# Cross-attention of layer 1: the DMA engines turn the high half of two tiles of each batch instead of one

## The chip, the cores and the metric

One core of a Trainium2 chip runs the whole program. The metric is the time of one launch on the device in microseconds (us), the median of several runs. Everything below is read from one profiled execution of the kernel before: its own time, its span from the first to the last instruction, and its trace. TensorE appears in it as PE (matmuls) and PEld (weight loads), VectorE as DVE, ScalarE as ACT, GpSimd as POOL, and the queue from which the DMAs are issued (SyncE) as SPq.

## The reference

Two layers of a gated cross-attention block over x of 16 x 56 x 128 and a context of 16 x 1500 x 128. Only the second layer's attention matters here:

```python
# 16 heads of 64, b = 16 batches, lq = 56 queries, lk = 1500 keys
Q = (X @ Wq.T + bq).reshape(b, lq, h, d)
KV = (encoder_out @ Wkv.T + bkv).reshape(b, lk, h, 2 * d)
K, V = (KV[..., :d], KV[..., d:])
scores = jnp.einsum('bqhd,bkhd->bhqk', Q, K) / SCALE
weights = jax.nn.softmax(scores, axis=-1)
attn = jnp.einsum('bhqk,bkhd->bqhd', weights, V).reshape(b, lq, h * d)
out = attn @ Wo.T + bo
```

Layer 0 has an attention of its own and an expert MLP, and layer 1 ends with a quantised MLP. All of it is the same before and after the change.

## The kernel before, in words

**Tiles.** A batch of layer 1 has 16 heads x 56 queries = 896 rows, cut into 7 tiles (T1) of 128 rows, against 1500 keys in 12 chunks of 125. A "group" is a set of tiles whose product with the context is made together: `GROUPS1` is tiles 0 to 3 and tiles 4 to 6. There are 16 batches, so 112 tiles.

**One tile.** PE makes the scores (`pe_scores1`, nine matmuls, L892) into three of the PSUM banks, two sets in turns. DVE takes the row maximum (`dve_max1`, L1573, then a small add, L1577). ACT takes the exponential into `e_row` (`act_exp1`, L1269) and sums the rows. The float32 exponentials are split in two float16 halves: POOL casts the high half (`pool_high1`, L585), and DVE subtracts it to get the low half (`dve_low1`, L1600). Both lie in `halves1`, a ring of two buffers by the tile's parity (named u_w and wg_sb in the trace, whose memory they use). The product with the context wants the halves with keys on the partitions, so both must be transposed, "turned", into `p1[group]`.

**The low halves** are turned by DMA transposes, one for each tile, issued from SyncE in `sync_turn1` (L449). For the first tile of a group SyncE first waits for `pv_done1`: the product of the same group of the batch before must have finished reading `p1[group]`, which the transpose overwrites. After that it waits for `low_done1` of the tile.

**The high halves** are turned by PE, twice six transposes against the identity (`pe_turn1`, L860, u = 0 and 1) into one PSUM bank, and copied out by ACT in two copies (`act_high1`, L1278). The exception is `BY_DMA`, tile 4, the first of the second group: a second DMA transpose turns it, issued right behind the tile's low half (L453), and PE and ACT skip it.

**Rings.** `pool_high1` of tile t writes the buffer of tile t - 2, so it waits until PE has turned that tile. For tile 6 (`BY_DMA + 2`) it waits for the DMA instead, semaphore `high_by_dma1`.

**Order on the engines.** The loop of layer 1 runs over batches and steps t = 0 to 6, written out by hand. In step t, PE makes the scores of tile t + 1, turns the high half of tile t - 1 and does a part of a group's product (`pe_pv1`, L912): the first group's 12 chunks lie in steps 5 and 6 and in steps 0 and 1 of the next batch, the second group's in steps 2 to 4. In step 1 all of the part comes before the second six transposes. Step 4, like step 0, begins behind the scores with a small transpose of the row sums' inverses (`pe_inverse1`, L884), which waits for both ACT copies of the tile turned in the step before. In step 6 of every second batch PE also makes a projection (L868). DVE's order in step t is: in steps 2 and 5 the scaling of a finished product (`dve_scale1`, L1591), then maximum of tile t + 1, reciprocal of the sum of tile t (L1582), low half of tile t. ACT's order in step t is: first copy of tile t - 1, exponential of tile t + 1, second copy of tile t - 1. POOL only casts, tile after tile. SyncE's order: low half of each tile as above, and between them the inverses' way to DRAM and back (L461, L469), the next batch's context (L423, L430).

**How long.** Layer 1's attention runs from about 640 to 1190 us of the span. A pair of batches takes some 68 us: in the pair that serves as the pattern here, step 1 of the first batch begins at 817.34 us and step 2 at 821.86 us, and step 2 of the second one at 853.93 us.

Of the kernel before, what the change touches and what calls it, by code (L numbers as in the profile page):

```python
# [27 lines left out]
def flamingo_kernel(nc, x, ctx_in, mask, g_xattn, g_ffn,  # L28
                    wv0, wk0, wq0, wo0, bo0, gate_w, sh_gate, sh_up, sh_down, rt_gate, rt_up, rt_down,
                    wq1, bq1, wkv1, bkv1, wo1, bo1, w_gate, w_up, w_down, out):  # L30
    B, S, E = x.shape
# [20 lines left out]
    T1 = ROWS // 128  # L52
# [17 lines left out]
    with ctx:  # L70
# [158 lines left out]
        GROUPS1 = [(0, 4), (4, T1)]  # L229
# [199 lines left out]
            part = slice(4 * third, 4 * third + 4)  # L429
            sp.dma_start(c_keep1[par][:, part], split_rows[b, :, part]).then_inc(sem(f"kept1_{par}"), 16)  # L430

        BY_DMA = GROUPS1[1][0]

        def turns_till(b, t):

            return b * (T1 - 1) + (t if t <= BY_DMA else t - 1)

        def turned1(b, par, t):

# [2 lines left out]
        def sync_turn1(sp, b, par, t):  # L442

            grp = 0 if t < GROUPS1[1][0] else 1
            first = GROUPS1[grp][0]
            if t == first:
                wait_apart(sp, "sp", (sem("pv_done1"), 4 * (b - 1) + 2 * grp + 2))
            wait_apart(sp, "sp", (sem("low_done1"), b * T1 + t + 1))
            sp.dma_start_transpose(p1[grp][:, 1, :, 128 * (t - first):128 * (t - first + 1)],  # L449
                                   halves1[(t + par) % 2][:, 1].rearrange("p c k -> p (c k)"))\  # L450
                .then_inc(turned1(b, par, t)[0], 16)
            if t == BY_DMA:
                sp.dma_start_transpose(p1[grp][:, 0, :, 128 * (t - first):128 * (t - first + 1)],  # L453
                                       halves1[(t + par) % 2][:, 0].rearrange("p c k -> p (c k)"))\
                    .then_inc(sem("high_by_dma1"), 16)
# [124 lines left out]
        def pool_high1(pool, b, par, t):  # L580

            wait_apart(pool, "pool", (sem("exp_done1"), b * T1 + t + 1), (sem("turned_high1"), 2 * turns_till(b, t - 1)))
            if t == BY_DMA + 2:
                wait_apart(pool, "pool", (sem("high_by_dma1"), 16 * (b + 1)))
            pool.tensor_copy(halves1[(t + par) % 2][:, 0, :, 0:KP], e_row[(t + par) % 2][:].rearrange("p (c k) -> p c k", c=KC))\  # L585
                .then_inc(sem("high_done1"), 1)

# [262 lines left out]
        def pe_turn1(pe, b, par, t, u, after_proj=False):  # L850

            if u == 0:
                pe.wait_ge(sem("high_done1"), b * T1 + t + 1)
            wait(pe, sem("high_copied1"), 2 * turns_till(b, t) + u)
            if after_proj:
                pe.wait_ge(sem("block_done1"), b)
            if isinstance(b, int) and b == B - 1 and t in (3, BY_DMA + 1) and u == 0:
                pe.wait_ge(sem("residual"), 2 * TT + (4 if t == 3 else EARLY))
            for c in range(UC):
                last = pe.transpose(turned_half1()[:, 128 * c:128 * (c + 1)], halves1[(t + par) % 2][:, 0, UC * u + c, :],  # L860
                                    ident16[:])
            last.then_inc(sem("turned_high1"), 1)
# [34 lines left out]
        def pe_pv1(pe, b, par, grp, first, end):  # L897

            a, z = GROUPS1[grp]
            cols = 128 * (z - a)  # L900
            if first == 0:
                for t in (z - 2, z - 1):
                    pe.wait_ge(*turned1(b, par, t))
                pe.wait_ge(sem("high_copied1"), 2 * turns_till(b, z))
                if grp == 1:
                    pe.wait_ge(sem("high_by_dma1"), 16 * (b + 1))
                wait(pe, sem("u_scaled1"), 2 * b + grp)
                if grp == 0:
                    pe.wait_ge(sem(f"kept1_{par}"), per_use(b, par, 48))
            for c in range(first, end):  # L910
                for cl, pl in ((0, 0), (0, 1), (1, 0)):
                    last = pe.matmul(bank[:, U_BANK, 0:cols], c_keep1[par][:, c, cl, :], p1[grp][0:KP, pl, c, :],  # L912
                                     start=(c == 0 and cl + pl == 0), stop=(c == KC - 1 and cl == 1))
                if c in (UC - 1, KC - 1):
                    last.then_inc(sem("pv_done1"), 1)

        @block.tensor
        def _(pe):
# [221 lines left out]
            def layer1(b, par, first, last):  # L1140
                for t in range(T1):
                    if t < T1 - 1:
                        pe_scores1(pe, b, par, t + 1)
                    elif not last:
                        pe_scores1(pe, b + 1, 1 - par, 0)
                    turn = (b, par, t - 1) if t > 0 else (b - 1, 1 - par, T1 - 1)
                    has_turn = not (first and t == 0) and t - 1 != BY_DMA
                    proj = t == T1 - 1 and par == 0 and not first
                    if t >= 5:
                        product = (b, par, 0, 3 * (t - 5), 3 * (t - 4))  # L1150
                    elif t < 2:
                        product = (b - 1, 1 - par, 0, 3 * (t + 2), 3 * (t + 3))
                    else:
                        product = (b - 1, 1 - par, 1, 4 * (t - 2), 4 * (t - 1))
                    has_product = t >= 5 or not first
                    middle = product[4] if t == 1 else product[3] + (3 if t in (0, 4) else 2)
                    if t == 0 and not first:
                        pe_inverse1(pe, b - 1, 1 - par, 1)
                    if t == 4:
                        pe_inverse1(pe, b, par, 0)  # L1160
                    if t in (0, 4) and has_product:
                        pe_pv1(pe, *product[:4], product[3] + 1)
                        product = (*product[:3], product[3] + 1, product[4])
                    if t == 4 or t == 0 and not first:
                        pe.wait_ge(sem("inverse_row1"), 2 * b + t // 4)
                    if proj:
                        pe.wait_ge(sem("high_copied1"), 2 * turns_till(b, t - 1))
                        pe_proj1(pe, b)
                    elif has_turn:
                        pe_turn1(pe, *turn, 0)  # L1170
                    if has_product:
                        pe_pv1(pe, *product[:4], middle)
                    if has_turn:
                        pe_turn1(pe, *turn, 0 if proj else 1, proj)
                    if has_product and middle < product[4]:
                        pe_pv1(pe, *product[:3], middle, product[4])
                    if proj:
                        pe_turn1(pe, *turn, 1)
                    if last and t in (3, 4):
                        pe.wait_ge(sem("high_copied1"), 2 * turns_till(b, t))  # L1180
                        pe_block_turn(pe, B - 2, range(4) if t == 3 else range(4, EARLY), early_turned, "block_done1")
# [90 lines left out]
        def act_high1(act, b, par, t, u):  # L1272
            grp = 0 if t < GROUPS1[1][0] else 1
            at = t - GROUPS1[grp][0]
            act.wait_ge(sem("turned_high1"), 2 * turns_till(b, t) + u + 1)
            if t in (0, BY_DMA + 1):
                wait(act, sem("pv_done1"), 4 * (b - 1) + 2 * grp + u + 1)
            act.copy(p1[grp][:, 0, UC * u:UC * (u + 1), 128 * at:128 * (at + 1)],  # L1278
                     turned_half1().rearrange("p (c r) -> p c r", c=UC)).then_inc(sem("high_copied1"), 1)
# [19 lines left out]
        def _(act):  # L1299
# [149 lines left out]
            def layer1(b, par, first, last):  # L1449
                for t in range(T1):  # L1450
                    if t == 0 and not first:
                        act_inverse1(act, b - 1, 1)
                    if t == 4:
                        act_inverse1(act, b, 0)
                    turn = (b, par, t - 1) if t > 0 else (b - 1, 1 - par, T1 - 1)
                    has_turn = not (first and t == 0) and t - 1 != BY_DMA
                    proj = t == T1 - 1 and par == 0 and not first
                    if proj:
                        act_block1(act, b)
                    elif has_turn:  # L1460
                        act_high1(act, *turn, 0)
                    if t < T1 - 1:
                        act_exp1(act, b, par, t + 1)
                    elif not last:
                        act_exp1(act, b + 1, 1 - par, 0)
                    if proj:
                        act_high1(act, *turn, 0)
                    if has_turn:
                        act_high1(act, *turn, 1)
# [421 lines left out]
```

## Time and profile before

| | before |
|---|---|
| median of 3 runs | 1237.04 us (1234.59 to 1239.03) |
| the profiled execution, its own time | 1237.67 us |
| its span | 1235.9 us |
| PE busy | 1121.8 us, 91% of the span |
| DVE busy | 890.4 us, 72% |
| ACT busy | 674.8 us, 55% |
| POOL busy | 519.8 us, 42% |
| chain that ended last, by engine | PE 73%, DVE 12%, ACT 6% |
| turns of the high halves, L860 | PE 192 groups of six, ACT 192 copies of 794 ns |
| DMA transposes | 128, 3.8 to 3.9 us from issue to landing (median) |

In the timeline every row has its start in us from the span's beginning, the duration in us, the engine, the line, the operation, the output and input by the program's names, the count of instructions merged into the row, and in brackets the idle time just before it with what ended it. Matmuls are pipelined, so that the duration of a group on PE reaches some 0.2 us into the next one; the cost of a group on PE is the distance between starts. A row of SPq lasts as long as the queue is taken by the issue, not until the transfer lands.

### The profile page before, as it was taken

How to read it: one execution, taken by the hardware profiler on the slowest of the kernel's cores; microseconds unless marked ns; L12 is line 12 of the kernel's file. 1: busy time of each engine (PE TensorE's matmuls, PEld its weight loads, DVE VectorE, ACT ScalarE, POOL GpSimd, SP SyncE). 2: the span in 40 equal slices, each digit the busy share in tenths (PEclk: the TensorE clock that was granted, in tenths of full speed). 3: DMA queues.
4: the chain of work that ended last, by engine and by line, in shares of the span. 5: the costliest groups of instructions: out<-in, count | busy, mean ns of one | idle time of the engine just before them, and what ended most of it. 6: DMA issues, size and time to landing. Idle time of an engine off the chain costs nothing.

```text
span 1235.9 us, 27523 instructions
## 1 busy us (share of the span) xinstructions
PE 1121.8 (91%) x9862; PEld 639.0 (52%) x9864; DVE 890.4 (72%) x1242; ACT 674.8 (55%) x935; POOL 519.8 (42%) x352
## 2 busy tenths in 40 slices
PE   4789999999999979878887999999999999999984
PEld 2255556566665645634433555555555555555542
DVE  7766666666666673587787887878787878878768
ACT  2345555555555545545575656656565656566532
POOL 8546675666666653432213332322232322323220
PEclk9889999999999999699998999999999999999996
DMA  3456555545555461000006887868776776768640
GB/s 105 121 169 197 169 168 165 156 149 160 157 178 158 145 159 47 20 1 26 2 0 130 161 164 142 158 140 163 137 163 144 156 162 141 159 141 160 131 79 16
DMA packets 247351, 157.59 MB, mean 128 GB/s; under 512 B 209664, under 2 KB 220400, under 8 KB 247296
## 3 DMA queue, kind: packets, MB, share of 16 engines
q1 hardware_dynamic: 247008, 156.86, 54.1%
q8 instruction: 34, 0.56, 0.2%
q14 instruction: 21, 0.17, 0.0%
q10 hardware_dynamic: 288, 0.00, 0.0%
HBM read 62.23 MB, written 25.39 MB: 71 GB/s over the span
## 4 chain that ended last, share of the span: by engine, by line
PE 73%; DVE 12%; issue 7%; ACT 6%; DMA 1%; SPq 0%; POOL 0%; ACTq 0%; DVEq 0%; another core or an unknown queue 0%; POOLq 0%
PE bank L892 16%; PE bank L912 15%; PE bank L767 7%; PE bank L791 6%; PE bank L860 5%; PE bank L795 5%; PE bank L808 4%; DVE region L1716 2%; PE bank L868 2%; PE bank L934 2%; DVE neg_max L1573 2%; ACT region L1242 2%; DVE e_row L1534 2%; PE bank L1135 2%; PE bank L1097 2%
## 5 line engine op out<-in xcount | busy, mean ns | idle before, releaser
L1534 DVE CUSTOM_DVE_ANT_0 e_row<-bank,region 112x1500 f32<-112x1500 f32 x128 | 220.1, 1719 | 125.5 <-PE bank L767 124.2
L1242 ACT ACTIVATE region<-bank 125x896 f32<-125x896 f32 x192 | 176.0, 917 | 203.8 <-PE bank L795 203.7
L1573 DVE TENSOR_REDUCE neg_max<-bank 128x1 f32<-128x1500 f32 x112 | 192.6, 1720 | 111.8 <-PE bank L892 111.8
L892 PE MATMUL bank<-region 128*128 128x500 f16 x1008 | 235.3, 379 | 3.2 <-ACT e_row L1269 1.8
L1269 ACT ACTIVATE e_row<-bank,neg_shift 128x1500 f32<-128x1500 f32 x112 | 169.2, 1511 | 101.0 <-DVE neg_shift L1577 58.4
L1278 ACT COPY region<-bank 128x768 f16<-128x768 f16 x192 | 152.4, 794 | 72.3 <-PE bank L860 72.3
L585 POOL CAST u_w<-e_row 128x1500 f16<-128x1500 f32 x56 | 83.0, 1483 | 209.4 <-ACT e_row L1269 179.2
L585 POOL CAST wg_sb<-e_row 128x1500 f16<-128x1500 f32 x56 | 83.1, 1484 | 192.4 <-ACT e_row L1269 128.4
L892 PEld LDWEIGHTS bank<-region 128*128 (+1 forms) x1008 | 97.4, 98 | 108.0 <-issue 3.5
L791 PE MATMUL bank<-row_of,region 112*128 112x448 bf16 x384 | 137.8, 359 | 7.6 <-ACT region L1242 7.6
L795 PE MATMUL bank<-region 97*128 (+1 forms) x768 | 137.6, 260 | 0.0
L912 PE MATMUL bank<-region 125*128 125x384 f16 (+1 forms) x576 | 126.1, 352 | 0.0
L912 PE MATMUL bank<-region,g_w 125*128 125x384 f16 (+1 forms) x576 | 124.8, 352 | 0.2 <-DMA region<-wg_sb 0.2
L646 POOL TENSOR_SCALAR region<-region 112x1500 bf16<-112x1500 int32 x16 | 105.3, 6583 | 35.3 <-PE bank L795 29.2
L767 PE MATMUL bank<-region 96*128 96x500 f16 x384 | 105.9, 385 | 12.5 <-DVE neg_max L1534 6.8
L808 PE MATMUL bank<-region 125*32 125x112 f32 x3072 | 113.1, 266 | 0.0
L795 PEld LDWEIGHTS bank<-region 97*128 97x128 f16 x768 | 76.0, 99 | 43.3 <-issue 0.9
L1600 DVE TENSOR_TENSOR u_w<-e_row,u_w 128x1500 f16<-128x1500 f32 x56 | 95.7, 1709 | 3.2 <-DMA region<-u_w 1.6
L1600 DVE TENSOR_TENSOR wg_sb<-e_row,wg_sb 128x1500 f16<-128x1500 f32 x56 | 95.5, 1706 | 3.1 <-POOL wg_sb L585 3.0
L808 PEld LDWEIGHTS bank<-region 125*32 125x32 f32 x3072 | 67.7, 109 | 41.0 <-issue 34.6
L912 PEld LDWEIGHTS bank<-region,g_w 125*128 125x128 f16 x576 | 52.8, 97 | 38.8 <-issue 1.3
L912 PEld LDWEIGHTS bank<-region 125*128 125x128 f16 x576 | 52.9, 97 | 38.5 <-issue 1.1
(218 smaller groups left out, 1495.3 us busy)
## 6 DMA issues: line engine op xcount, KB each, us to landing
region<-region SPq DMA_DIRECT2D x192, 96.0 KB, 2.2
turned_rows<-region SPq DMA_DIRECT2D x16, 768.0 KB, 3.8
region<-turned_rows SPq DMA_DIRECT2D x32, 384.0 KB, 3.5
c_in<-in_ctx SPq DMA_DIRECT2D x16, 750.0 KB
split_rows<-region SPq DMA_DIRECT2D x16, 750.0 KB
region<-in_mask_Bx1xSxS_if SPq DMA_DIRECT2D x32, 328.1 KB
region<-split_rows SPq DMA_DIRECT2D x24, 250.0 KB
g_w<-split_rows SPq DMA_DIRECT2D x24, 250.0 KB
```

Of the source, the lines that this page charges most:

```text
L585: pool.tensor_copy(halves1[(t + par) % 2][:, 0, :, 0:KP], e_row[(t + par) % 2][:].rearrange("p (c k) -> p c k", c=KC))\
L767: last = pe.matmul(bank[:, k, 0:4 * KP], q0_flat[0:96, bass.ds(b * ROWS + R0 * t, 128)], c_stack[par][0:96, t // 2, 4 * k:4 * k + 4, 0:KP] ...
L791: pe.matmul(into[:, 0:HALF_ROWS], mask_flat[par][:, KP * c:KP * c + 128], row_of[:].rearrange("p h s -> p (h s)"), start=True, stop=False)
L795: last = pe.matmul(into[:, GC * g:GC * (g + 1)], c_stack[par][0:97, 2 * h + g, c, :], q0[0:97, b, rows:rows + GC], start=False, stop=(g == 1))
L808: pe.matmul(bank[32 * j:32 * j + 32, U_BANK, 0:R0], c_pv[par][:, c, 4 * h + j, :], p0[:, c, R0 * j:R0 * (j + 1)], start=(c == 0), stop=False)
L892: last = pe.matmul(score_banks1(par, t)[:, k, :], q1[:, ql, b, 128 * t:128 * (t + 1)], c_t1[par][:, cl, 4 * k:4 * k + 4, 0:KP], start=(ql ...
L912: last = pe.matmul(bank[:, U_BANK, 0:cols], c_keep1[par][:, c, cl, :], p1[grp][0:KP, pl, c, :], start=(c == 0 and cl + pl == 0), stop=(c = ...
L1242: act.activation(p0[:, 2 * i:2 * i + 2, :], ring0("s", h, i)[0:KP, :, 0:HALF_ROWS], ACT.Exp, scale=SCALE0)\
L1269: act.activation(e_row[(t + par) % 2][:].rearrange("p (a k) -> p a k", a=3), score_banks1(par, t), ACT.Exp, bias=neg_shift[:, t:t + 1], ac ...
L1534: dve.tensor_tensor_reduce(out=masked.rearrange("p (a k) -> p a k", a=3), in0=bank[0:R0, 0:3, 0:4 * KP], in1=mask_bias[par][:].rearrange(" ...
L1573: dve.tensor_reduce(neg_max[:, t:t + 1], score_banks1(par, t), AX.XY, ALU.max, negate=True)\
L1600: dve.tensor_tensor(half[:, 1, :, 0:KP], e_row[(t + par) % 2][:].rearrange("p (c k) -> p c k", c=KC), half[:, 0, :, 0:KP], ALU.subtract).t ...
```

## The change

`BY_DMA` becomes a list of the first tile of each group, tiles 0 and 4. So tile 0's high half, too, is turned by a DMA transpose that SyncE issues right behind that of its low half. PE's twelve transposes and ACT's two copies for tile 0 go away, the counts of turned tiles follow (5 for each batch instead of 6), POOL's cast of tile 2 waits for the DMA of tile 0 as that of tile 6 does for tile 4, the first group's product waits for the DMA as well, and ACT's wait for free space in `p1[0]` moves from tile 0 to tile 1. The order of everything else is kept.

```diff
-        BY_DMA = GROUPS1[1][0]
+        BY_DMA = [first for first, _ in GROUPS1]
         def turns_till(b, t):
-            return b * (T1 - 1) + (t if t <= BY_DMA else t - 1)
+            return b * (T1 - len(BY_DMA)) + t - len([d for d in BY_DMA if d < t])
+        def turned_by_dma(b, grp):
+            return sem("high_by_dma1"), 16 * (b * len(BY_DMA) + grp + 1)
@@ sync_turn1
-            if t == BY_DMA:
+            if t in BY_DMA:
                 sp.dma_start_transpose(p1[grp][:, 0, :, 128 * (t - first):128 * (t - first + 1)],
                                        halves1[(t + par) % 2][:, 0].rearrange("p c k -> p (c k)"))\
                     .then_inc(sem("high_by_dma1"), 16)
@@ pool_high1
-            if t == BY_DMA + 2:
-                wait_apart(pool, "pool", (sem("high_by_dma1"), 16 * (b + 1)))
+            if t - 2 in BY_DMA:
+                wait_apart(pool, "pool", turned_by_dma(b, BY_DMA.index(t - 2)))
@@ pe_pv1
-                if grp == 1:
-                    pe.wait_ge(sem("high_by_dma1"), 16 * (b + 1))
+                pe.wait_ge(*turned_by_dma(b, grp))
@@ the loops of PE and ACT
-                    has_turn = not (first and t == 0) and t - 1 != BY_DMA
+                    has_turn = not (first and t == 0) and t - 1 not in BY_DMA
@@ act_high1
-            if t in (0, BY_DMA + 1):
+            if t - 1 in BY_DMA:
                 wait(act, sem("pv_done1"), 4 * (b - 1) + 2 * grp + u + 1)
```

## Rows read from the trace of the kernel before

**Rows 1.** Windows: PE, PEld, DVE, ACT, POOL busy, then PEclk, DMA share, GB/s.
```profile
700.00:1170.00 470.00, 464.40 (x3097) 257.12 (x3096) 364.77 (x414) 284.38 (x393) 143.23 (x97) 1.00 0.76 151
```
**Rows 2.** Timeline, PE and SPq around step 1 of a batch (first of a pair).
```profile
817.34 2.08 PE L892 MATMUL bank<-region 128*128 128x500 f16 x9
...
819.25 0.50 PE L860 MATMUL bank<-ident,wg_sb 128*128 128x128 f16 x6
...
821.53 0.50 PE L860 MATMUL bank<-ident,wg_sb 128*128 128x128 f16 x6
821.86 2.08 PE L892 MATMUL bank<-region 128*128 128x500 f16 x9
...
821.95 1.32 SPq L449 DMA_TRANSPOSE region<-wg_sb  x1
...
823.46 1.77 SPq L449 DMA_TRANSPOSE region<-u_w  x1
```
**Rows 3.** Timeline, the same batch: tile 4's DMA transpose and POOL's cast of tile 6.
```profile
838.46 1.79 SPq L453 DMA_TRANSPOSE region<-wg_sb  x1
...
840.47 0.64 SPq L461 DMA_DIRECT2D inverse_rows<-place  x1
...
842.72 1.44 POOL L585 CAST wg_sb<-e_row 128x1500 f16<-128x1500 f32 x1 [4.22 <-DMA region<-wg_sb]
...
843.72 0.44 DVE L1577 TENSOR_TENSOR neg_shift<-neg_max,lift 128x1 f32<-128x1 f32 x1
...
844.19 1.72 DVE L1600 TENSOR_TENSOR wg_sb<-e_row,wg_sb 128x1500 f16<-128x1500 f32 x1
```
**Rows 4.** Timeline, a DMA transpose of tile 4 (batch 2) and the cast it released.
```profile
733.95 1.85 SPq L453 DMA_TRANSPOSE region<-u_w  x1
...
739.60 1.44 POOL L585 CAST u_w<-e_row 128x1500 f16<-128x1500 f32 x1 [5.32 <-DMA region<-u_w]
```
**Rows 5.** Timeline, steps 2 to 4 of the batch of rows 2.
```profile
823.25 1.44 POOL L585 CAST wg_sb<-e_row 128x1500 f16<-128x1500 f32 x1 [3.21 <-ACT e_row L1269]
...
827.77 1.44 POOL L585 CAST u_w<-e_row 128x1500 f16<-128x1500 f32 x1 [3.09 <-ACT e_row L1269]
...
828.44 0.50 PE L860 MATMUL bank<-ident,wg_sb 128*128 128x128 f16 x6
...
828.64 1.72 DVE L1573 TENSOR_REDUCE neg_max<-bank 128x1 f32<-128x1500 f32 x1 [1.06 <-PE bank L892]
...
831.15 2.08 PE L892 MATMUL bank<-region 128*128 128x500 f16 x9
...
833.07 0.27 PE L884 MATMUL bank<-ident,row_inv 128*4 128x128 f32 x1
```
**Rows 6.** Timeline, layer 0: two POOL instructions in a row, other buffers.
```profile
42.09 3.10 POOL L639 TENSOR_TENSOR region<-c_in,region 125x1536 f16<-125x1536 f32 x1
45.13 1.57 POOL L654 COPY region<-c_in 125x1536 f32<-125x1536 f32 x1
```
**Rows 7.** Timeline, batch 2, steps 2 to 4: a low half that came late.
```profile
723.05 1.72 DVE L1600 TENSOR_TENSOR u_w<-e_row,u_w 128x1500 f16<-128x1500 f32 x1 [1.59 <-DMA region<-u_w]
...
729.05 0.27 PE L884 MATMUL bank<-ident,row_inv 128*4 128x128 f32 x1 [0.40 <-ACT region L1278]
```
**Rows 8.** Timeline, steps 2 to 4 of the other kind of batch (second of a pair).
```profile
854.01 1.45 SPq L449 DMA_TRANSPOSE region<-u_w  x1
...
855.65 1.63 SPq L449 DMA_TRANSPOSE region<-wg_sb  x1
...
865.43 0.27 PE L884 MATMUL bank<-ident,row_inv 128*4 128x128 f32 x1
```
**Rows 9.** Timeline, PE in batch 0: nine score matmuls at the lower clock.
```profile
655.57 3.55 PE L892 MATMUL bank<-region 128*128 128x500 f16 x9
```
**Rows 10.** Windows as in rows 1: two stretches of batch 0 in which PE idles.
```profile
651.80:655.00 3.20, 0.49 (x6) 0.35 (x6) 3.17 (x5) 2.52 (x5) 1.44 (x1) 1.00 0.59 112
...
644.25:646.05 1.80, 0.00 (x0) 0.00 (x0) 1.77 (x3) 1.60 (x2) 0.00 (x0) 1.00 0.00 0
```

More of the change, by code:

```diff
@@ L856, in pe_turn1 @@
                 pe.wait_ge(sem("block_done1"), b)
-            if isinstance(b, int) and b == B - 1 and t in (3, BY_DMA + 1) and u == 0:
+            if isinstance(b, int) and b == B - 1 and t in (3, BY_DMA[1] + 1) and u == 0:
                 pe.wait_ge(sem("residual"), 2 * TT + (4 if t == 3 else EARLY))
@@ L1455, in layer1 @@
                     turn = (b, par, t - 1) if t > 0 else (b - 1, 1 - par, T1 - 1)
-                    has_turn = not (first and t == 0) and t - 1 != BY_DMA
+                    has_turn = not (first and t == 0) and t - 1 not in BY_DMA
                     proj = t == T1 - 1 and par == 0 and not first
```

## The prediction, as it was put on record before the run

> **What bounds the kernel now.** The page first: PE is busy for 91% of the span and holds 73% of the chain that ended last. Layer 1's attention can then be looked at alone in the windows: in 470 us of it PE is busy for 464.4 us, at the full clock, while DVE has 364.8, ACT 284.4 and POOL 143.2 us [rows 1]. So in this stage work taken off PE is time gained, as long as nothing makes PE wait. The reader should see one more thing there: PE has no idle time to give, so every us that it is made to wait is a us lost, and this is the side on which the change has to be judged. For that the timeline is the right view, step by step, and in it the order of SyncE, POOL and DVE around the tile whose turn moves.
>
> **What the change removes.** PE's cost of a group of six transposes is the distance from its start to the next start: 821.53 to 821.86, so 0.33 us [rows 2]. Tile 0 has two groups, 0.66 us for each batch. One stands before the end of the first group's product in step 1, the other behind it. Over 16 batches that is 10.6 us, all on PE, which bounds. ACT's two copies were beside PE's work (ACT has 284.4 of 470 us [rows 1]) and I count them at nothing: they are hidden by PE's scores and products, and without that cover they would be worth 0.8 us each by the table.
>
> **What it adds: an issue.** SyncE issues a second transpose behind tile 0's low half. The place matters. Tile 0's low half is not issued when it is ready but when `pv_done1` lets it, at the end of step 1: 821.95, beside the start of step 2 on PE at 821.86 [rows 2]. The added issue therefore starts at the end of step 1 as well. It takes the queue for some 2.0 us, as tile 4's does (838.46 to 840.47 [rows 3]). Queued behind it are tile 1's low half (before at 823.46 [rows 2], now some 1.7 us later), the inverses of the batch before and the next context. The next tile's low half that DVE makes comes several us later, by which time the queue is free again, so I count the issue itself at nothing; were that slack gone, the 2.0 us would be its price in a batch.
>
> **What it adds: a wait, and who stands behind it.** POOL's cast of tile 2 overwrites tile 0's high half and now waits for the DMA to land. For tile 4 the same wait ends 4.26 us after the issue begins (838.46 to 842.72 [rows 3]); the longest such distance is 5.65 us, in batch 2 [rows 4]. I take 4.26, which is that of the steady batches, and keep 5.65 for the range; the lower bound would be a landing that is there before POOL asks, a cost of nothing. For batch 0, whose `pv_done1` wait is void, I give 1 us in all.
>
> Step by step in the batch of rows 2, all starts as before up to 817.34:
> - The product ends 0.33 us sooner, so tile 0's low half is issued at 821.95 - 0.33 = 821.62 and the high half 1.51 us later (the distance of two neighbouring transposes, 821.95 to 823.46 [rows 2]), at 823.13.
> - It has landed, and POOL begins tile 2's cast, at 823.13 + 4.26 = 827.39. Before, it began at 823.25 [rows 5], with nothing to wait for. The cast ends at 828.83 (1.44 us).
> - Tile 3's exponential is ready by then: its cast stood at 827.77 before [rows 5]. So two casts follow each other on POOL, tile 2's and tile 3's. The casts' successors: DVE wants to make tile 2's low half as soon as the first one is done. In the trace DVE starts 0.03 us after the end of the cast (842.72 + 1.44 = 844.16, start 844.19 [rows 3]). POOL starts its next instruction, when its waits are long fulfilled, 0.06 us before the end of the one before by the modelled spans (42.09 + 3.10 = 45.19, start 45.13 [rows 6]). So POOL comes first.
> - A DVE instruction that comes second waits for POOL: the small add beginning at 843.72 lasts 0.44 us, to 844.16, exactly the end of the cast that runs beside it [rows 3]. So the low half cannot run beside tile 3's cast: 828.83 + 1.44 + 1.70 gives 831.97 for its end, rather than 830.56.
> - Behind the low half stand, on DVE, the maximum of tile 4, then on ACT its exponential and the second copy of tile 2, then on PE the small transpose L884 of step 4. That chain can be read where a low half came late: 723.05 + 1.72 = 724.77 to 729.05, so 4.28 us, and the row says that PE idled for ACT there [rows 7]. So L884 starts at 836.25, against 833.07 before [rows 5]: **3.18 us** later in this batch.
>
> In the other kind of batch the same steps give: 854.01 - 0.33 = 853.68, issue of the high half 1.64 us later at 855.32, landing 859.58, end of the second cast 862.46, low half 864.16, L884 at 868.44, against 865.43 [rows 8]: **3.01 us**. The mean is 3.1 us. The 0.66 us that PE saves lie within it, since they are before L884. From L884 on DVE is no longer late against PE: the maximum of tile 4 came at 828.64 only because it waited for PE [rows 5], and such waits take up the rest. The next batch starts as late as this one ended, and PE cannot win it back. 15 batches have the `pv_done1` wait: 15 x 3.1 = 46.5 us.
>
> **A page of the Trainium skill on this step.** "SBUF — State Buffer", section "Who interferes with whom", says that a DVE instruction with two SBUF inputs contends with a GpSimd instruction that reads SBUF, and that whoever issues first holds the shared ports for the whole instruction. The low half has two such inputs and the cast reads SBUF; the small add of rows 3 agrees. By this rule the sum stays at 3.1 us a batch; without any contention it would be the 1.7 us of the first rival.
>
> **What it adds: the clock.** PE idles within the batch: turn of tile 2 at 828.9 instead of 828.44 [rows 5], then the scores of tile 5 at 828.9 + 2.71 (828.44 to 831.15) = 831.6, over at 833.5 (831.15 to 833.07), and nothing to do until 836.25, some 2.7 us. In batch 0 a stretch of 3.20 us with 0.49 us of PE work was followed by nine score matmuls in 3.55 us at the lower of the two clock levels, 1.2 instead of 2.4 GHz, against 2.08 us [rows 9, 2]: 1.47 us lost. A stretch of 1.80 us with no work kept the clock [rows 10]. Our 2.7 us lie between, so the price of a batch is between 0 and 1.47 us; nearer to the longer one, but I take half, 0.7 us: 15 x 0.7 = 10.5 us.
>
> **The sum.** 46.5 + 10.5 + 1 = 58 us on the profiled execution's own 1237.67 us (span 1235.9 and 1.8 around it), which stands 0.6 us above the median: 1237.04 + 58 = **1295 us**.
>
> **The rivals.**
> - **DVE comes before POOL** at the hand-over. Then the low half ends at 830.56 and L884 starts at 834.84, 1.77 us late; 1.60 us in the other kind; mean 1.7. The idle stretch is 1.3 us, short enough to keep the clock [rows 10]. 15 x 1.7 = 25.5, with batch 0 1264 us. For it: only 0.1 us separates the two starts, and the POOL row is from another stage. Against it: all else in the trace has POOL's waits served ahead.
> - **The landing is hidden, and the kernel gets faster.** The place is POOL's wait before tile 2's cast. L884 stays at 833.07 if the low half ends by 828.79, so if the high half lands by 828.79 - 1.70 - 1.44 = 825.6, that is 2.5 us after its issue at 823.13. Below that the 0.66 us begin to count; if the landing is early enough, 16 x 0.66 = 10.6 us are gained: 1226 us. It would also need DVE and ACT to keep up with the shorter step. For it: tile 4's turn by DMA costs PE nothing, since its low half is issued early in its step. Against: every landing in rows 3 and 4 took over 4 us.
> - **The landing is as slow as in batch 2** in every batch, since tile 1's transpose is issued close behind: 1.39 us more, 15 x 1.39 = 21 us, 1316 us. Against it: tile 1's transpose stands behind in the same queue.
> - **Nothing to be seen**, as the wait costs just what PE saves: within 0.3%, that is 1233 to 1241 us. It needs a landing some 2.5 us after the issue in every batch, for which no row speaks.
> - That the change does not remove the turns is no rival: the loops of PE and ACT skip tile 0 by the same test that skips tile 4.
>
> **How the numbers follow.** POOL first, with the clock's cost anywhere between none and full (1285 to 1307 us): 0.64. DVE first: 0.20. Slower landing: 0.05. Hidden: 0.07. Nothing to be seen: 0.04. A difference of about 0.3% is what a measurement of this kernel can tell from no change; so slower 0.89, same 0.04, faster 0.07. The range for 8 in 10 runs from the DVE-first case, 1260, to the full price of the clock with some of the slower landing, 1312.
>
> **What the profile after would show.** POOL's cast of tile 2 released by the DMA in every batch, some 4 us later against the end of step 1. The cast of tile 3 directly behind it; DVE's low half of tile 2 with some 3.1 us instead of 1.7 if POOL comes first, 1.7 if not. PE's idle time before L884 of the first group some 2.7 us (1.3 in the rival) and named as waiting for ACT, and about 0.5 to 1 us before the turn of tile 2. Nine-matmul groups of over 3 us if the clock falls. Steps 5, 6, 0 unchanged, step 1 shorter by 0.66 us. The prediction is wrong if the high half lands within 2.5 us, or if `pv_done1` is not what holds the first issue back.

## The result, and the profile after

| | before | after |
|---|---|---|
| median | 1237.51 us (1234.59 to 1239.03, 4 runs) | 1293.38 us (1291.48 to 1305.89, 4 runs) |
| the profiled execution, its own time | 1237.67 us | 1295.08 us |
| its span | 1235.9 us | 1293.4 us |
| PE busy | 91% | 87% |
| chain that ended last: PE, DVE, DMA | 73%, 12%, 1% | 60%, 13%, 5% |

The ratio is 1.0462, with a 95% interval of 1.0408 to 1.0516: the change makes the kernel 4.6% slower. One of the five runs of experiment 2 below took 1614.97 us at a granted clock of 0.65, where the others have 0.97, and is left out of its ratio. The line numbers after are 3 to 4 higher than before (L884 is now L888, L892 is L896, L585 is L589, L912 is L915).

The window that rows 1 show, in the kernel after (columns as there):

```profile
700.00:1170.00 470.00, 424.42 (x2641) 229.01 (x2638) 341.08 (x377) 240.99 (x332) 125.04 (x88) 0.97 0.74 148
```

PE is busy for 424 of 470 us instead of 464, and no other engine has taken its place: all of them do less in the same time. So the engines wait for each other, and the waits of PE, with total, number and longest, name for whom in that window:

```profile
PE bank L888 <- ACT region L1281: 30.5, 14, 2.4
PE bank L864 <- POOL u_w L589: 5.1, 6, 1.1
PE bank L864 <- POOL wg_sb L589: 4.9, 6, 0.8
...
PE bank L915 <- DVE region L1594: 2.4, 12, 0.2
```

L888 is the small transpose of the row sums' inverses. Thirteen of its fourteen waits lie in step 4, one for each batch of the window, and take 2.22 to 2.39 us each; the other, 1.02 us, lies in step 0 once. Before, this wait was 1.6 us in all. ACT is only the last link. The timeline of a batch shows the whole chain (first kind, to be laid beside rows 2 and 5; step 1 begins at 835.80):

```profile
835.80 2.08 PE L896 MATMUL bank<-region 128*128 128x500 f16 x9
...
840.08 1.44 SPq L453 DMA_TRANSPOSE region<-wg_sb  x1
...
841.57 1.80 SPq L457 DMA_TRANSPOSE region<-wg_sb  x1
...
845.87 1.44 POOL L589 CAST wg_sb<-e_row 128x1500 f16<-128x1500 f32 x1 [7.36 <-DMA region<-wg_sb]
...
847.25 1.44 POOL L589 CAST u_w<-e_row 128x1500 f16<-128x1500 f32 x1
847.34 2.92 DVE L1603 TENSOR_TENSOR wg_sb<-e_row,wg_sb 128x1500 f16<-128x1500 f32 x1 [3.33 <-POOL wg_sb L589]
847.45 0.51 PE L864 MATMUL bank<-ident,wg_sb 128*128 128x128 f16 x6 [0.82 <-POOL wg_sb L589]
...
850.18 1.71 DVE L1576 TENSOR_REDUCE neg_max<-bank 128x1 f32<-128x1500 f32 x1
...
854.46 0.27 PE L888 MATMUL bank<-ident,row_inv 128*4 128x128 f32 x1 [2.22 <-ACT region L1281]
```

Read from the top: SyncE issues the low half where the product lets it, then the high half; POOL has idled 7.36 us when that has landed; two casts follow each other without a gap, DVE's low half starts 0.09 us behind the second and needs 2.92 us instead of 1.70; maximum, exponential and copy follow; PE has idled 2.22 us at L888. From the start of step 1 to L888 it takes 18.66 us, against 15.73 us before (817.34 to 833.07 [rows 2, 5]): 2.93 us more. In the other kind of batch it is 872.10 to 890.82, 18.72 us against 16.03 us (849.40 to 865.43 [rows 8]): 2.69 us more.

The rest lies behind L888, and only in the first kind, in PE's work of step 4:

```profile
855.50 2.03 PE L915 MATMUL bank<-region 125*128 125x384 f16 x6
857.33 0.85 PE L864 MATMUL bank<-ident,u_w 128*128 128x128 f16 x6
857.97 1.17 PE L915 MATMUL bank<-region 125*128 125x384 f16 x3
```

In the second kind the same three take 1.14, 0.51 and 0.65 us. The granted clock, the number before the last two, is at its lower level from 856 to 859 us and back behind it:

```profile
856.00:859.00 3.00, 3.00 (x15) 1.78 (x14) 1.29 (x1) 2.79 (x4) 0.66 (x1) 0.50 0.92 204
859.00:860.00 1.00, 1.00 (x6) 0.46 (x5) 0.56 (x1) 0.01 (x1) 0.78 (x1) 0.99 0.00 0
```

From L888 to step 1 of the next batch it takes 17.64 us (854.46 to 872.10) against 16.33 us before (833.07 to 849.40): 1.31 us more. In the second kind it is 20.14 against 20.15 us. So a pair of batches costs 2.93 + 1.31 + 2.69 = 6.93 us more. The distances of L888 say the same: 75.2 us for a pair (36.4 and 38.8) against 68.25.

From the first L888 of a group-0 product to the last it is 567.8 us against 512.8: 55.0 of the 57.4 us that the two profiled executions differ by. What stands ahead of the first (batch 0) is 2.7 us longer and what stands behind the last is not longer (59.4 against 59.6 us).

### The profile page after: what moved, and what is told of

Its sections match the earlier page's. It is cut to its first block, busy times and chain, and to the rows that moved or that the text cites. A ratio compares the mean times of both kernels' runs of the same rounds, so it can differ in the third digit from the quotient of the medians.

```text
span 1293.4 us, 27104 instructions
## 1 busy us (share of the span) xinstructions
PE 1128.8 (87%) x9672; PEld 635.1 (49%) x9672; DVE 905.5 (70%) x1242; ACT 650.8 (50%) x903; POOL 515.1 (40%) x352
## 4 chain that ended last, share of the span: by engine, by line
PE 60%; DVE 13%; issue 11%; ACT 6%; DMA 5%; POOL 2%; SPq 2%; DVEq 0%; ACTq 0%; POOLq 0%
PE bank L915 12%; PE bank L896 9%; PE bank L771 7%; PE bank L795 5%; PE bank L799 5%; PE bank L812 4%; PE bank L864 3%; DMA region<-wg_sb 3%; DVE neg_max L1576 3%; DMA region<-u_w 3%; DVE e_row L1537 2%; DVE region L1719 2%; ACT region L1245 2%; PE bank L872 2%; PE bank L937 2%
## 5 line engine op out<-in xcount | busy, mean ns | idle before, releaser
L896 PE MATMUL bank<-region 128*128 128x500 f16 x1008 | 236.9, 381 | 3.3 <-ACT e_row L1272 1.8
L589 POOL CAST u_w<-e_row 128x1500 f16<-128x1500 f32 x56 | 80.6, 1439 | 233.9 <-ACT e_row L1272 174.8
L589 POOL CAST wg_sb<-e_row 128x1500 f16<-128x1500 f32 x56 | 81.8, 1461 | 228.2 <-DMA region<-wg_sb 101.7
L1281 ACT COPY region<-bank 128x768 f16<-128x768 f16 x160 | 127.2, 795 | 72.6 <-PE bank L864 72.5
L896 PEld LDWEIGHTS bank<-region 128*128 (+1 forms) x1008 | 98.4, 99 | 113.5 <-issue 6.2
L915 PE MATMUL bank<-region 125*128 125x384 f16 (+1 forms) x576 | 134.1, 369 | 1.6 <-DVE region L1594 1.6
L915 PE MATMUL bank<-region,g_w 125*128 125x384 f16 (+1 forms) x576 | 125.9, 354 | 1.4 <-DVE region L1594 1.4
L1603 DVE TENSOR_TENSOR wg_sb<-e_row,wg_sb 128x1500 f16<-128x1500 f32 x56 | 105.2, 1878 | 27.7 <-POOL wg_sb L589 27.7
L1603 DVE TENSOR_TENSOR u_w<-e_row,u_w 128x1500 f16<-128x1500 f32 x56 | 104.9, 1873 | 26.9 <-POOL u_w L589 26.9
L915 PEld LDWEIGHTS bank<-region 125*128 125x128 f16 x576 | 55.8, 102 | 45.3 <-issue 7.7
L915 PEld LDWEIGHTS bank<-region,g_w 125*128 125x128 f16 x576 | 53.4, 98 | 42.5 <-DVE region L1594 2.2
```

Of the source, the lines that this page charges most:

```text
L896: last = pe.matmul(score_banks1(par, t)[:, k, :], q1[:, ql, b, 128 * t:128 * (t + 1)], c_t1[par][:, cl, 4 * k:4 * k + 4, 0:KP], start=(ql ...
L1603: dve.tensor_tensor(half[:, 1, :, 0:KP], e_row[(t + par) % 2][:].rearrange("p (c k) -> p c k", c=KC), half[:, 0, :, 0:KP], ALU.subtract).t ...
```

## The experiments

The ratios are to the kernel before.

**1. The hand-over from POOL to DVE.** POOL's cast of tile 3 waits, in the changed kernel, until DVE has made tile 2's low half.

```diff
+            if t == 3:
+                wait_apart(pool, "pool", (sem("low_done1"), b * T1 + 3))
             pool.tensor_copy(halves1[(t + par) % 2][:, 0, :, 0:KP],
...
```

> The changed kernel, and POOL's cast of tile 3 also waits until DVE has made tile 2's low half, so that DVE comes first at the hand-over. Theory (the time lies in POOL's wait for the landing, 1.4 us a batch more in the hand-over, and some 0.65 us a batch in the clock that the long idle stretch costs): the low half takes 1.7 instead of 2.9 us, L888 idles about 0.9 instead of 2.3 us, the clock holds; 15 x 1.4 + 10 = 31 us less than the changed kernel's 1293, so 1262. Rival (the order at the hand-over is hidden, the landing alone counts): no change, 1293.

Measured: 1264.01 us, ratio 1.0222 (1.0189 to 1.0254). 29 us of the 56 are gone by adding a wait. The low half and L890 (L888 there) of the same kind of batch:

```profile
835.11 1.72 DVE L1605 TENSOR_TENSOR wg_sb<-e_row,wg_sb 128x1500 f16<-128x1500 f32 x1 [3.36 <-POOL wg_sb L591]
...
837.00 1.44 POOL L591 CAST u_w<-e_row 128x1500 f16<-128x1500 f32 x1 [1.93 <-DVE wg_sb L1605]
...
841.03 0.27 PE L890 MATMUL bank<-ident,row_inv 128*4 128x128 f32 x1 [1.02 <-ACT region L1283]
```

The idle time before L890 is 1.02 and 1.19 us in the two kinds. From L890 to L890 a pair of batches takes 71.3 us (33.7 and 37.6) instead of 75.2, and no groups at the lower clock are left in the steady batches; 15 x 3.9 / 2 = 29 us. So the order at the hand-over, with the clock that hangs on it, makes half the loss: that is shown.

**2. The wait on POOL.** Tile 0's high half is cast into a buffer of its own, which nobody overwrites in the same batch. Both transposes are issued where they were.

```diff
         carve([128, KC, 2, E], F16)
+        spare_high = region[:, split_at:split_at + KC * 64].bitcast(F16).rearrange("p (c k) -> p c k", c=KC)
...
+        def high1(par, t):
+            return spare_high if t == 0 else halves1[(t + par) % 2][:, 0]
@@ pool_high1
-            if t - 2 in BY_DMA:
+            if t == 0:
+                wait_apart(pool, "pool", turned_by_dma(b - 1, 0))
+            if t - 2 in BY_DMA[1:]:
...
```

The cast, the subtraction and the transpose of tile 0 then take `high1(par, t)` as their buffer.

> The changed kernel, but tile 0's high half lies in a buffer of its own, so that POOL's cast of tile 2 has nothing to wait for; both DMA transposes, their place in the queue and the product's wait for them stay. Theory (only the wait costs): PE keeps the 0.66 us a batch, less some 0.2 us in which step 2's product now waits for DVE's scaling; 1237.5 - 15 x 0.46 to 0.66 = 1227 to 1231. Rival (the second transpose itself costs, by traffic or by holding SyncE's queue): 1250 or more.

Measured: 1225.81 us, ratio 0.9904 (0.9878 to 0.9931). The same kernel again, with more runs:

> The changed kernel with tile 0's high half in a buffer of its own once more, in more rounds, for the interval: 1226 us, ratio 0.990 to the kernel before.

Measured: 1226.62 us, ratio 0.9905 (0.9874 to 0.9936). The transposes cost nothing; the wait on POOL was the whole loss and more. The window of rows 1 in this kernel, and PE's waits in it:

```profile
700.00:1170.00 470.00, 459.87 (x2971) 251.33 (x2969) 369.31 (x424) 269.43 (x371) 141.43 (x98) 1.00 0.82 164
```

```profile
PE bank L922 <- DVE region L1601: 2.7, 14, 0.2
...
PE bank L895 <- ACT region L1288: 1.3, 6, 0.3
```

PE is back at 460 us, the DMA share rose to 0.82, and L895 (L888 there) waits 1.3 us in all. What is left is a wait of 0.2 us a batch for DVE's scaling in step 2.

**3. The removal alone.** Tile 0's high half is turned by nobody (its place in `p1` holds zeros), and neither POOL nor the product waits for it.

```diff
@@ sync_turn1
-            if t in BY_DMA:
+            if t == 4:
                 sp.dma_start_transpose(p1[grp][:, 0, ...
@@ pool_high1
-            if t - 2 in BY_DMA:
+            if t - 2 == 4:
...
@@ pe_pv1
-                pe.wait_ge(*turned_by_dma(b, grp))
+                if grp == 1:
+                    pe.wait_ge(*turned_by_dma(b, 1))
...
```

> The changed kernel without tile 0's high transpose and without any wait for it: tile 0's high half is turned by nobody (its place in p1 holds zeros), so that this is the removal alone. Theory: 1227 to 1231, within 2 us of the kernel with the buffer of its own, since the issue and the traffic of the transpose are hidden. Rival (issue and traffic cost something): this kernel is faster than that one by over 4 us.

Measured: 1226.83 us, ratio 0.9912 (0.9882 to 0.9942), the same as experiment 2 within the intervals. So the issue on SyncE and the 384 KB through the DMA engines are hidden, as far as a difference of about 4 us in all, or 0.25 us a batch, can be told.

**4. The high half first.** Tile 0's two transposes change places in the queue.

```diff
+            def low():
+                sp.dma_start_transpose(p1[grp][:, 1, :, 128 * (t - first):128 * (t - first + 1)],
...
+            if t != 0:
+                low()
             if t in BY_DMA:
                 sp.dma_start_transpose(p1[grp][:, 0, :, 128 * (t - first):128 * (t - first + 1)],
...
+            if t == 0:
+                low()
```

> The changed kernel with tile 0's high half issued ahead of its low half. The high half lands 1.5 us sooner, the low half (for which DVE's low half of tile 2 waits, being in the same buffer) 1.5 us later. Theory: POOL casts tile 2 some 1.5 us sooner; if tile 3's exponential is ready by then, POOL again comes first and the gain is 15 x 1.5 + 10 for the clock = 32 us, 1261; if DVE comes first, 15 x 2.9 + 10 = 53 us, 1240. Rival (POOL's wait is not what binds): 1293.

Measured: 1249.28 us, ratio 1.0104 (1.0072 to 1.0136), between the two numbers of the theory. The timeline shows both of its cases, one in each kind of batch:

```profile
861.70 1.72 DVE L1608 TENSOR_TENSOR u_w<-e_row,u_w 128x1500 f16<-128x1500 f32 x1 [1.63 <-DMA region<-u_w]
861.97 2.75 POOL L594 CAST wg_sb<-e_row 128x1500 f16<-128x1500 f32 x1 [0.54 <-ACT e_row L1277]
...
867.70 0.27 PE L893 MATMUL bank<-ident,row_inv 128*4 128x128 f32 x1 [0.44 <-ACT region L1286]
...
897.88 1.44 POOL L594 CAST u_w<-e_row 128x1500 f16<-128x1500 f32 x1 [0.44 <-ACT e_row L1277]
897.97 2.92 DVE L1608 TENSOR_TENSOR wg_sb<-e_row,wg_sb 128x1500 f16<-128x1500 f32 x1 [1.91 <-DMA region<-wg_sb]
...
905.09 0.27 PE L893 MATMUL bank<-ident,row_inv 128*4 128x128 f32 x1 [1.78 <-ACT region L1286]
```

In the first DVE comes 0.27 us before POOL, needs 1.72 us, and POOL's cast stretches to 2.75; PE idles 0.44 us. In the second POOL comes 0.09 us before DVE, which needs 2.92 us, and PE idles 1.78 us. PE's idle time differs by 1.3 us between the kinds, and in the second one POOL's lead was only 0.09 us. The kinds differ in more than the order, though; the next experiment gives both the same order.

**5. Both orders together:** the edits of experiments 1 and 4.

> The changed kernel with both orders changed: tile 0's high half issued ahead of its low half, and POOL's cast of tile 3 behind DVE's low half of tile 2. With the high half first alone 1249 us was measured, POOL coming first in one kind of batch (2.92 us low half, 1.78 us idle before L888) and DVE in the other (0.45 us idle). Theory: both kinds behave like the second one, so the pair takes some 1.2 us less and the clock holds: 1249 - 8 x 1.2 = 1239. Rival (the two orders do not add): 1249 or more.

Measured: 1238.07 us, ratio 0.9991 (0.9966 to 1.0016). In the kind in which POOL had come first:

```profile
973.86 1.72 DVE L1610 TENSOR_TENSOR wg_sb<-e_row,wg_sb 128x1500 f16<-128x1500 f32 x1 [1.90 <-DMA region<-wg_sb]
...
979.79 0.27 PE L895 MATMUL bank<-ident,row_inv 128*4 128x128 f32 x1 [0.58 <-ACT region L1288]
```

The low half takes 1.72 instead of 2.92 us, and PE idles 0.58 instead of 1.78 us (0.44 in the other kind, as before), so the order alone makes 1.2 us on PE. A pair of batches takes 68.2 us (911.61 to 979.79), as in the kernel before: what PE saves pays for what is left of the waits. The profiled execution took 1247.81 us, at the upper end; the 10 us lie ahead of this stage, where the first of these transposes stands at 670.88 us and in experiment 4 at 660.91.

**6. No high half by DMA at all,** `BY_DMA = []`, PE turning tile 4 too.

> No high half is turned by DMA: tile 4 goes back to PE as well. This measures the price of a tile's turn on PE, and what tile 4's DMA transpose (the kernel before) had brought. Theory (0.66 us of PE a tile, nothing else bound): 1237.5 + 16 x 0.66 = 1248. Rival (a part of the turn is hidden behind other work): under 1243.

Measured: 1247.91 us, ratio 1.0082 (1.0059 to 1.0104), 10.5 us over the 1237.40 us of the kernel before beside it. The turn of a tile costs PE 0.66 us a batch, as rows 2 had it.

**7. Another tile instead of tile 0:** `BY_DMA = [2, 4]` and `BY_DMA = [1, 4]`, with the counts of the waits following.

> Tiles 2 and 4 are turned by DMA instead of 0 and 4, tile 0 by PE again. Tile 2's low half does not wait for the product, only for DVE, so the high half should land some 2 us after POOL could cast tile 4, as tile 4's own does for tile 6, and DVE asks for that cast some 1.5 us later still. Theory (the place decides: a landing that is late against the end of a product): the wait costs under 0.3 us a batch, 1226 to 1231. Rival (any second tile by DMA puts a wait on POOL that PE pays for): 1250 or more.

Measured: 1235.70 us (10 runs from 1231.59 to 1248.29), ratio 1.0000 (0.9968 to 1.0033). A miss for both: no loss, but the gain is not there either.

> Tiles 1 and 4 are turned by DMA, tile 0 by PE. Tile 1's pair of transposes stands behind tile 0's low half at the same late place of SyncE's queue, so its high half is issued about 1.7 us later than tile 0's was and lands some 2.3 us after POOL could cast tile 3; but the next maximum, tile 5, lies a whole step later against DVE's other work. Theory (a wait on POOL of 2 to 2.5 us is absorbed, one of 4 us is not): 1226 to 1232. Rival (as long as the pair is issued behind the end of the product, PE pays): 1245 or more.

Measured: 1245.18 us, ratio 1.0082 (1.0036 to 1.0128). Here the rival was right: L890 idles 0.9 to 1.0 us in ten of the 16 batches. The hand-over has another form here. POOL has idled 4.88 us before tile 3's cast, against 3.09 us [rows 5], and DVE's small add, which needs 0.16 us elsewhere, begins just behind it and lasts until it ends:

```profile
904.65 1.44 POOL L591 CAST u_w<-e_row 128x1500 f16<-128x1500 f32 x1 [4.88 <-PE bank L866]
904.69 1.40 DVE L1582 TENSOR_TENSOR neg_shift<-neg_max,lift 128x1 f32<-128x1 f32 x1
```

For tile 2 the profiled execution (1248.29 us, at the upper end of its runs) is long for a reason ahead of this stage: its first L890 comes at 673.54 us, where the kernel before has it at 663.54. From its first L890 of a group-0 product to its last it takes 514.0 us, against 512.8 in the kernel before and 503.5 in experiment 2, so the gain is missing in this stage itself. The same machinery shows at another place, with POOL's late cast of tile 4:

```profile
847.74 1.44 POOL L591 CAST wg_sb<-e_row 128x1500 f16<-128x1500 f32 x1 [4.50 <-DMA region<-wg_sb]
...
848.28 0.90 DVE L1582 TENSOR_TENSOR neg_shift<-neg_max,lift 128x1 f32<-128x1 f32 x1
```

Step 5's product then idles, by 5.2 us in all in twelve waits. The profile names ACT's copy for these, but that had ended 0.3 us before in one of them (815.71, against 816.04); the landing of tile 3's low half is an argued cause, not a shown one.

**8. Three tiles by DMA,** 0 from a buffer of its own, 2 and 4 from the ring.

> Three tiles by DMA: tile 0 from a buffer of its own (no wait on POOL), tiles 2 and 4 from the ring. Theory (PE bounds and each tile is worth 0.66 us a batch until DVE, with some 3.7 us of work a step, is reached): 1225.8 - 16 x 0.66 = 1215, up to 1221 if the steps shortened to 3.9 us make PE wait for DVE. Rival (a third transpose overloads the DMA engines): 1226 or more.

Measured: 1263.25 us, ratio 1.0245 (1.0178 to 1.0311). This looks like the overload of the rival. But the timeline shows the changed kernel's pattern once more, now for tiles 4 and 5, with PE's waits in the window behind it:

```profile
838.92 1.44 POOL L598 CAST wg_sb<-e_row 128x1500 f16<-128x1500 f32 x1 [5.84 <-DMA region<-wg_sb]
...
840.30 1.44 POOL L598 CAST u_w<-e_row 128x1500 f16<-128x1500 f32 x1
840.39 2.92 DVE L1612 TENSOR_TENSOR wg_sb<-e_row,wg_sb 128x1500 f16<-128x1500 f32 x1 [2.07 <-POOL wg_sb L598]
...
843.88 3.01 PE L924 MATMUL bank<-region,g_w 125*128 125x512 f16 x9 [2.73 <-DVE region L1603]
```

```profile
PE bank L924 <- DVE region L1603: 35.8, 26, 3.5
```

**9. Three tiles, all from two buffers outside the ring,** each with a semaphore of its own for the landings. The transposes stay as in experiment 8 and the waits on POOL go, which tells the waits from the load on the DMA engines.

```diff
+            if t not in BY_DMA:
+                return halves1[(t + par) % 2][:, 0]
+            return spares[(len(BY_DMA) * par + BY_DMA.index(t)) % 2]
@@ pool_high1
+            if t in BY_DMA:
+                ready, count = turned_by_dma(b, par, BY_DMA.index(t))
+                wait_apart(pool, "pool", (ready, count - 16))
...
```

> Three tiles by DMA (0, 2 and 4) as in the kernel before that had three, but every one of them from a buffer outside the ring (two buffers in turns), so that POOL has no landing to wait for in the next two tiles. DMA traffic and SyncE's issues are the same as in that kernel, which took 1263 us. Theory (the wait on POOL and the hand-over to DVE behind it, not the third transpose, cost the 37 us against the kernel with one own buffer): 1225.8 - 16 x 0.66 = 1215, up to 1222 where the shorter steps make PE wait for DVE. Rival (DMA load or SyncE's queue): 1240 or more.

Measured: 1235.27 us (10 runs from 1230.98 to 1245.66), ratio 0.9987 (0.9947 to 1.0026). 28 us less than experiment 8 with the same transposes, so the waits on POOL were that loss. But 1215 us was missed. PE's waits in the window show the next limit:

```profile
PE bank L928 <- DMA region<-wg_sb: 10.7, 7, 2.1
PE bank L928 <- DMA region<-u_w: 5.9, 6, 1.5
```

The product of the first group begins in step 5 and needs tile 3's low half turned. Behind tile 2's two transposes that one stands later in SyncE's single queue: DVE has made the low half at 826.41 us and it is issued at 827.68, 1.27 us later, where in the kernel before it was 0.11 us (832.24 to 832.35). The thirteen waits, together 16.6 us, are more than the 10.6 us that the third tile was to bring.

**10. Two tiles, both from buffers outside the ring,** the same code with `BY_DMA = [0, 4]`.

> Tiles 0 and 4 by DMA as in the changed kernel, both from buffers outside the ring: also tile 4's wait on POOL is gone. Theory: tile 4's wait, 1.0 us past the time POOL asks, is covered by slack, so no gain over the kernel that takes tile 0 alone out of the ring: 1226 within 3 us. Rival (it costs a little in every batch): 1220 or less.

Measured: 1224.03 us, ratio 0.9879 (0.9838 to 0.9921). Its interval overlaps that of experiment 2, so tile 4's wait was all but covered. This is the fastest kernel of the study, and like experiment 2 clear of the kernel before: the change, with the wait taken away.

## Why the prediction was right, step by step

1295 us was put on record, with 1260 to 1312; 1293.38 us was measured. The mechanism was the forecast one. That the number is within 2 us is in part luck: of the 58 us of the sum, the delay was put 4 us too high, and batch 0 and the batches outside the pattern some 4 us too low, against 57.4 us between the two profiled executions.

- **What PE saves**, 0.66 us a batch: right. Step 1 takes 3.86 instead of 4.52 us (835.80 to 839.66, 817.34 to 821.86). Experiment 6 has 10.5 us for 16 tiles against the 10.6 of the sum, and experiment 3 the same from the other side (11 us less than before).
- **The place of the issue**, at the end of step 1 behind `pv_done1`: right. It comes 4.28 us after the start of step 1, as worked out (817.34 to 821.62).
- **The landing** 4.26 us after the issue: 4.30 us in the first kind (841.57 to 845.87) and 4.42 us in the second (877.73 to 882.15). It is 4.29 to 4.45 us in all batches but two, 5.40 us in batch 1 and 4.73 us in batch 2. Right; the 5.65 us of rows 4 was not the pattern, and the rival on it falls.
- **POOL first at the hand-over**: right, in each of the 16 batches. The low half took 2.92 or 2.83 us. The row of layer 0 on which this rested [rows 6] held here. The rival's number for DVE first, 1264 us, is what experiment 1 measured when DVE was made first.
- **The delay of L888**: 2.93 and 2.69 us against the forecast 3.18 and 3.01. The terms were a little too large. In the first kind the low half ends 14.46 us after the start of step 1, not 14.63: the two casts stand 1.38 us apart and not 1.44, and the low half ends 1.57 us behind the second cast and not 1.70. The chain behind it took 4.20 and not 4.28 us. In the second kind the two issues stand 1.36 us apart and not 1.64. 15 x 2.8 = 42 us, where 46.5 was the term.
- **The clock**: the term was 0.7 us a batch, as half of 1.47. From batch 3 on it falls in every second batch, for 1.31 us: 0.66 us a batch. The size was right, the picture less so. It was the product of step 4 just behind the wait that ran slow (nine score matmuls did only in batch 0 and in the last one, 3.55 us at 1230.65), and the two kinds differ although PE idles 2.22 us before L888 in the one that loses the clock and 2.30 us in the one that keeps it. In batch 2 it fell behind 2.30 us of idle time as well (granted 0.50 from 739.6 to 742.9 us). So the length of this stretch alone does not decide it, and what does is not shown by these runs.
- **PE's idle time** before L888 was put at 2.7 us and is 2.2 to 2.3; before the turn of tile 2 it is 0.8, within the 0.5 to 1 us.
- **The issue at nothing**: right, by experiments 2 and 3 (1225.8 and 1226.8 us).
- **Batch 0**, 1 us: what stands ahead of its L888 is 2.7 us longer. Too small a guess.
- **Outside the pattern**: 42, 10 and 2.7 us make some 55 of the 57.4. From L888 to L888 it takes 1.5 us more than the pattern out of batch 2 and into the last batch, the two in which the clock fell in addition.
- **Not in the sum**: in step 2 the product waits 0.2 us for DVE's scaling, since step 1 on PE has become shorter. It is hidden in the changed kernel, as PE must wait further on in any case, and shows in experiment 2.
- **The rival on the faster side**, a hidden landing at 1226 us: it did not happen, but its price is what experiment 2 measured with the wait taken away.

On one of these steps a rule bears. The Trainium skill's page "SBUF — State Buffer", section "Who interferes with whom", has whoever issues first hold the shared ports for the whole instruction; experiment 4 agrees on both sides of the line, DVE at 2.92 us behind POOL and POOL at 2.75 us behind DVE.

Where my later expectations failed: after 1264 and 1226 us had come out to the us, I took 2 us of waiting on POOL for covered, from the one place where it was (tile 4). For tile 1 it was not, and for tile 2 the freed time was lost elsewhere.

## What to carry to other kernels

Work moved off the bounding engine to a DMA costs nothing in itself, as long as nobody must wait for its landing. Ask who overwrites its source: a buffer that came free behind two short passes of TensorE is held until the DMA has landed, 4.3 us behind its issue, and the in-order engines behind the wait carry it back to the one that bounds. Before taking such a change back, look for a buffer to take the source out of the ring: here 3 KB a partition turned a loss of 4.6% into a gain of 1.0%.

When an engine is held back until it has two instructions ready, look at who comes first: here POOL ran both without a gap in all 16 batches, ahead of DVE, which waited for the first.

## What the runs showed of the hardware that I had not expected

- A wait added to POOL made the kernel 29 us faster (experiment 1): two casts from float32 in a row had stretched DVE's subtraction, which reads two SBUF operands, from 1.7 to 2.9 us in each batch, and without that the clock held in the steady batches too.
- The same code came out one way in one kind of batch and the other way in the other (experiment 4): DVE first by 0.27 us, POOL first by 0.09 us.
- From batch 3 to batch 14 the lower clock came steadily in the batches with 2.22 us of idle time on PE before L888 and not in those with 2.29 to 2.38 us, though it did in batch 2 with 2.30 us. It stayed for some 3.4 us (855.60 to 859.01).
